# Routing logits transposed, attention logits by two blocks, and a software pipeline written out at both ends

## What is computed

```python
x = x + attention(layernorm(x))
x = x + slots(layernorm(x))
# attention, per batch
q    = tanh(x @ W_charge.T + b);  shell = normalised(x @ W_shell.T + b)
phi  = (powers 0..4 of q, outer product with cos/sin of shell @ omega.T) @ W_combine.T   # 64 features
attn = softmax(causal(phi @ phi.T * decay / temp));  out = attn @ V @ W_out.T
# slots, per batch
h      = gelu(concat(x, slot_mean) @ w1.T + b1)
logits = (h @ w2.T + b2) / (|tau| + 0.1)            # 64 per token
alpha  = softmax over the 8 largest of the 64, 0 elsewhere
S_new  = GRU(alpha.T @ x / sum(alpha), slots);  out = alpha @ (S_new @ wv.T + bv) @ wo.T
```

## Time and profile before

| what | us |
|---|---|
| median of 3 runs (809.03 to 813.24) | 812.28 |
| the profiled execution's own time | 810.81 |
| its span, first to last instruction | 809.0 |
| PE busy | 736.9 (91%) |
| DVE busy | 614.1 (76%) |
| ACT busy | 438.8 (54%) |
| POOL busy | 420.4 (52%) |
| mean granted clock of TensorE | 0.969 of full speed |

### The profile page before, as it was taken

One profiled execution on the slowest core, in us unless ns is written; L12 is line 12 of the kernel. 1 busy time (PEld: TensorE's weight loads), 2 busy tenths in 40 slices (PEclk: granted clock), 3 DMA queues, 4 the chain that ended last, 5 costly groups with the idle time before them and its releaser, 6 DMA issues.

```text
span 809.0 us, 14937 instructions
## 1 busy us (share of the span) xinstructions
PE 736.9 (91%) x4448; PEld 584.9 (72%) x4448; DVE 614.1 (76%) x2069; ACT 438.8 (54%) x870; POOL 420.4 (52%) x681
## 2 busy tenths in 40 slices
PE   4647799999999999999999999999999999989952
PEld 2535576878778787878787787878787877767742
DVE  1653769697888979797979889797979798866642
ACT  0414648383847656473838475664737384727310
POOL 1433465656473837566564738374665557361410
PEclk9978999999999999999999999999999999999976
DMA  8015352535463544546454535445464645262133
GB/s 288 6 34 123 79 131 53 131 91 145 116 144 106 133 140 111 166 105 184 92 144 124 141 113 127 145 112 155 106 182 97 167 108 151 53 156 77 57 104 104
DMA packets 80104, 97.11 MB, mean 120 GB/s; under 512 B 12118, under 2 KB 54680, under 8 KB 80024
## 3 DMA queue, kind: packets, MB, share of 16 engines
q1 hardware_dynamic: 75760, 92.95, 44.6%
q10 hardware_dynamic: 4264, 3.20, 1.3%
HBM read 20.62 MB, written 16.78 MB: 46 GB/s over the span
## 4 chain that ended last, share of the span: by engine, by line
PE 67%; DVE 8%; DMA 5%; POOL 5%; SPq 5%; ACT 5%; issue 4%; ACTq 0%; POOLq 0%; DVEq 0%
PE ps L341 13%; PE ps L262 13%; PE ps L236 12%; PE ps L367 6%; PE ps L408 4%; PE ps L297 3%; PE ps L393 3%; POOL Z L1079 2%; PE ps L314 2%; DMA X<-in_x 2%; SPq L1244 2%; DMA out_x<-X 2%; PE ps L316 2%; PE ps L230 2%; PE ps L379 2%
## 5 line engine op out<-in xcount | busy, mean ns | idle before, releaser
L341 PE MATMUL ps<-VS,ET 128*128 128x257 f32 x640 | 160.3, 389 | 0.0
L341 PEld LDWEIGHTS ps<-VS,ET 128*128 128x128 f32 x640 | 114.3, 191 | 25.5 <-DVE X L803 10.5
L610 ACT ACTIVATE E<-ps,nmax 128x128 f32<-128x128 f32 (+3 forms) x128 | 66.2, 532 | 86.1 <-DVE nmax L791 85.5
L726 DVE TENSOR_TENSOR VS<-ps,biasM 128x354 f32<-128x354 f32 x128 | 67.0, 524 | 42.2 <-PE ps L262 40.2
L1079 POOL TENSOR_TENSOR Z<-Z,QB 128x512 f32<-128x512 f32 x64 | 81.7, 1276 | 32.0 <-ACT Z L591 29.3
L549 ACT ACTIVATE xn<-X,rs 128x256 f32<-128x256 f32 x128 | 66.3, 590 | 40.1 <-POOL rs L1029 39.9
L262 PE MATMUL ps<-W1h,xh 128*128 128x354 f32 x256 | 86.5, 338 | 0.7 <-DVE xl L715 0.7
L262 PE MATMUL ps<-W1h,xl 128*128 128x354 f32 x256 | 83.6, 326 | 0.0
L262 PE MATMUL ps<-W1l,xh 128*128 128x354 f32 x256 | 83.3, 325 | 0.0
L631 ACT ACTIVATE xmT<-ps 128x512 f32<-128x512 f32 x64 | 36.7, 608 | 78.9 <-PE ps L236 78.9
L791 DVE TENSOR_REDUCE nmax<-ps 128x1 f32<-128x128 f32 (+3 forms) x128 | 60.6, 483 | 21.3 <-PE ps L318 21.0
(11 more groups left out here) (176 smaller groups left out, 1873.7 us busy)
## 6 DMA issues: line engine op xcount, KB each, us to landing
X<-in_x SPq DMA_DIRECT2D x32, 512.0 KB, 4.8
xmT<-Z SPq DMA_DIRECT2D x128, 128.0 KB, 2.3
out_x<-X SPq DMA_DIRECT2D x32, 512.0 KB, 3.6
QS<-Z SPq DMA_DIRECT2D x64, 128.0 KB, 2.4
KH<-Z SPq DMA_DIRECT2D x64, 128.0 KB, 2.4
KL<-Z SPq DMA_DIRECT2D x64, 128.0 KB, 2.4
AS<-grz SPq DMA_DIRECT2D x32, 128.0 KB, 2.4
AS<-aTl SPq DMA_DIRECT2D x32, 128.0 KB, 2.4
```

What stands on the lines that cost most here:

```text
L341: ins = e.matmul(p[:, 0:D + 1], ET[:, r % 2, j * 128:j * 128 + 128], VS[:, (2 * k + d) % 4, j, 0:D + 1], start=j == 0, stop=j == i)
L610: e.activation(E[:, r % 3, 0:w], at["lg", r][:, 0:w], ACT.Exp, bias=nmax[:, r % 8:r % 8 + 1]).then_inc(s["E"], 1)
L726: e.tensor_tensor(VS[:, b % 4, t, :], at["vs", b, t][:, 0:FEATS], biasM[:, :], ALU.add).then_inc(s["vs"], 1)
```

## The change

- **Routing.** `route` is one step for a pair: w2 is stationary and the hidden layer moves, two matmuls with 512 columns, one to each half of the partitions. `rt_out` (ACT) adds the bias, `rt_t` (PE) transposes the result with four transposes into a bank of ring T. `top` and `shift` read the logits there; `route_logits` is gone. `shift` of the logits moves from POOL to DVE, and that of the 8 maxima stays on POOL (`shift8`).
- **Attention logits.** `logits(k, n)` makes two blocks: four fp32r matmuls, then two mask matmuls.
- **phi.** The last two matmuls use all 128 rows, with weights `w4` in which one half is zero.
- **Norms.** The DVE's bn_aggr instructions (16 for a pair) go; `ln_scale` and `lm_scale` join the two halves that bn_stats leaves, with four more small POOL instructions in each.
- **Order.** All sequences are new. The loop runs over `range(3, NP - 1)`; what comes before and after it is written out. The first batches' statistics stand ahead of the weight setup on DVE, the first transposes ahead of the bias setup on PE; the loads of the slot layer move from ACT's queue to SP's.
- A few waits and small forms are added or changed.

```diff
-        SETUP, SOFT, CHAIN, SLOTS = 9, 9, 5, 12
+        SETUP, SOFT, CHAIN, SLOTS = 7, 9, 5, 12
...
-                    ins = e.matmul(p[own(d), :], wc[own(d), 2, :], Z[own(d), 4, :], start=False, stop=True)
+                    ins = e.matmul(p[own(d), :], w4[:, d, :], Z[:, 4, :], start=False, stop=True)
...
             def logits(k, n):
+                for r in (8 * k + 2 * n, 8 * k + 2 * n + 1):
+                    at["lg", r], before = L.take(s["E"], r + 1)
+                    if before:
+                        e.wait_ge(*before)
                 if n == 0:
                     e.wait_ge(s["qk"], 192 * (k + 1))
+                for u in (2 * n, 2 * n + 1):
+                    d, i = divmod(u, 4)
+                    rows, wide = slice(i * 128, i * 128 + 128), max(i * 128 + 128, 256)
+                    p = at["lg", 8 * k + u]
+                    for j, keys in enumerate((KH, KL)):
+                        e.matmul(p[:, 0:wide], QS[:, d, rows], keys[:, d, 0:wide], start=j == 0, stop=False,
+                                 skip_group_check=True)
+                for u in (2 * n, 2 * n + 1):
+                    i = u % 4
+                    e.matmul(at["lg", 8 * k + u][:, i * 128:i * 128 + 128], identb[:, :], maskb[:, :], start=False,
+                             stop=True, skip_group_check=True).then_inc(s["lg_mm"], 1)
...
-                for t in range(4):
-                    ins = e.matmul(p[:, t * S:t * S + S], hT[:, d, t * 128:t * 128 + 128], w2[:, :],
-                                   start=True, stop=True, skip_group_check=True)
+                e.wait_ge(s["h"], 2 * k + 2)
+                for d in range(2):
+                    ins = e.matmul(p[own(d), :], w2[:, :], hT[:, d, :], start=True, stop=True)
                 ins.then_inc(s["rt_mm"], 1)
+            def rt_t(k):
+                p, before = T.take(s["dm"], 2 * k + 2)
+                e.wait_ge(s["rtT"], k + 1)
+                transposes(p, [RT[:, t * 128:t * 128 + 128] for t in range(4)]).then_inc(s["rt_t"], 1)
...
+            def rt_out(k):
+                e.wait_ge(s["rt_mm"], k + 1)
+                e.activation(RT, at["rt", k][:, :], ACT.Identity, bias=b2[:, 0:1]).then_inc(s["rtT"], 1)
...
+                e.tensor_tensor(lg[:, d, 0, :, :], logits_of(k, d),
+                                m8[:, d, :, 0:1].broadcast_to([128, 4, S]), ALU.subtract).then_inc(s["dm"], 1)
...
+            for it in range(3, NP - 1):
+                p, n, f, m, g = it + 2, it + 1, it, it - 1, it - 2
+                e_t(f, 5); values(f, 4); xn_t(p, 0, 0); e_t(f, 6); values(f, 5); xn_t(p, 0, 1); phi(n)
+                e_t(f, 7); values(f, 6); values(f, 7); xn_t(p, 1, 0); xn_t(p, 1, 1); out_mm(g, 0, 0)
+                proj(p, 0, 0); out_mm(g, 0, 1); gather(m); proj(p, 0, 1); out_mm(g, 1, 0); proj(p, 0, 2)
+                proj(p, 0, 3); proj(p, 1, 0); proj(p, 1, 1); out_mm(g, 1, 1); proj(p, 1, 2); proj(p, 1, 3)
+                logits(n, 0); gi_t(m); xm_t(f, 0, 0); xm_t(f, 0, 1); gx_rz(m); logits(n, 1); e_t(n, 0)
+                e_t(n, 1); gx_n(m); q_t(p); xm_t(f, 1, 0); xm_t(f, 1, 1); hidden(f, 0); hidden(f, 1)
+                values(n, 0); al_t(m); logits(n, 2); route(f); values(n, 1); z_t(p); e_t(n, 2); slot_v(m)
+                rt_t(f); values(n, 2); e_t(n, 3); e_t(n, 4); logits(n, 3); values(n, 3)
```

More of the change, by code:

```diff
@@ L83 @@
 ln_r ln_b
+rt_t rtT wcast
+ln_d ln_e ln_q lm_d lm_e lm_q
 """.split()
@@ new lines, in _ @@
+            e_t(1, 2); logits(1, 2); values(1, 1); xm_t(0, 1, 0); xn_t(3, 0, 1); e_t(1, 3); xm_t(0, 1, 1)
+            values(1, 2); hidden(0, 0); hidden(0, 1); z_t(2); e_t(1, 4); values(1, 3); logits(1, 3)
+            route(0); proj(3, 0, 0); values(1, 4); rt_t(0); e_t(1, 5); proj(3, 0, 1); e_t(1, 6); phi(2)
+            values(1, 5); proj(3, 0, 2); proj(3, 0, 3); xn_t(3, 1, 0); e_t(1, 7); values(1, 6)
+            xn_t(3, 1, 1); values(1, 7); proj(3, 1, 0); proj(3, 1, 1); proj(3, 1, 2); logits(2, 0)
@@ new lines, in _ @@
+            gather(0); xm_t(1, 0, 0); proj(3, 1, 3); gi_t(0); e_t(2, 0); logits(2, 1); gx_rz(0); q_t(3)
+            values(2, 0); e_t(2, 1); xm_t(1, 0, 1); gx_n(0); e_t(2, 2); logits(2, 2); xm_t(1, 1, 0)
+            xm_t(1, 1, 1); hidden(1, 0); hidden(1, 1); logits(2, 3); al_t(0); route(1); values(2, 1)
+            e_t(2, 3); rt_t(1); values(2, 2); z_t(3); e_t(2, 4); slot_v(0); values(2, 3); xn_t(4, 0, 0)
+            values(2, 4); e_t(2, 5); xn_t(4, 0, 1); xn_t(4, 1, 0); e_t(2, 6); values(2, 5); e_t(2, 7)
@@ new lines, in _ @@
+            phi(3); proj(4, 0, 0); proj(4, 0, 1); values(2, 6); xn_t(4, 1, 1); proj(4, 0, 2); proj(4, 0, 3)
+            out_mm(0, 0, 0); values(2, 7); xm_t(2, 0, 0); out_mm(0, 0, 1); proj(4, 1, 0); proj(4, 1, 1)
+            proj(4, 1, 2); proj(4, 1, 3); logits(3, 0); gather(1); out_mm(0, 1, 0); out_mm(0, 1, 1); q_t(4)
+            xm_t(2, 0, 1); gi_t(1); logits(3, 1); gx_rz(1); e_t(3, 0); xm_t(2, 1, 0); xm_t(2, 1, 1); gx_n(1)
+            hidden(2, 0); hidden(2, 1); values(3, 0); e_t(3, 1); e_t(3, 2); logits(3, 2); al_t(1)
```

497 lines of the change are left out of this document (308 added, 189 removed).

## The result

The changed kernel takes 780.12 us (median of four runs, 776.68 to 782.99), the kernel before 810.65 in the same session (808.04 to 813.24). The ratio is 0.962, with a 95% interval from 0.957 to 0.968: 3.8% faster, and 3 us from the predicted 777. The profiled execution of after took 776.68 us with a span of 774.9, that of before 810.81 with 809.0, so the spans differ by 34.1 us, where the prediction's terms sum to 35. After's profiled execution is the fastest of its four, so what is read from its trace describes a time 3.4 us under the median.

What follows compares the result with a forecast made beforehand. PE work was taken to bound the middle (44.24 us a turn), latencies both ends. Middle -15, start -17 and end -3 bring 810.8 to 775.8; the median stands 1.5 above, so 777 us, range 768 to 786 (chance 0.50).

Steps and rivals of the forecast that it cites:

- The start: Up to the logits of pair 1: earlier statistics and transposes, `proj` woven into idle PE time; -17 us.
- the weaving of `proj(2)`: Between the logits of pairs 0 and 1: `proj(2)` fills idle PE time in pair 0's attention; 6 us.
- Rival D: At the start: latencies of one pair are only moved, -7 in place of -17, 787 us; chance 0.12.
- Rival B: Middle turns lose their short gaps too, 1.7 us each, and the start gives 24: 761 us; chance 0.15.
- Sum: -1.05 us a pair: PE work in a middle turn: fp32r entries -0.63, routing -0.36, phi -0.06, masks and the rest 0.
- the price of 0 for the gaps of the old turn: Middle turns on PE: old gaps against waiting for two ring L banks, 0, between -0.8 and +0.8 a turn.
- the terms of phi and of the routing: PE in a middle turn: phi's last two matmuls -0.06 us, routing from 1.8 to 1.44, -0.36.
- The entries: PE in a middle turn: seven fewer switches into fp32r at 0.09 us each, -0.63.
- The bank wait: `e_t(f, 5)` on PE waits for ring T's bank until DVE's `shift`; 0.8 us of room, priced 0, up to 3.
- Rival C: Middle: DVE reaches `top` late by more than 0.8 us, holding up PE every turn; slower, 829 us; chance 0.06.
- Ring L's two banks: Two-block logits on PE wait for two free banks instead of one; 0, between -0.8 and +0.8 a turn.
- The end: Last pair: `gather` goes ahead of `out_mm` and starts 2.5 us sooner; -3 in all, between -6 and +3.

Runs made afterwards that it cites:

- this mixture: Changed kernel with the routing part and phi's last two matmuls in their old forms, in the new order: 793.7 us, ratio 0.979 to before.
- the dose: Changed kernel with four unused reductions on DVE ahead of `top`, 2.3 us more DVE time a turn: 796.0 us, ratio 0.983 to before.
- the last experiment: Changed kernel with `z_t` ahead of the slot setup's rest and some first- and last-pair moves issued from ACT's queue: 779.1 us, ratio 0.961 to before.

## Why the prediction was right, and where two errors met

**The sum and its parts.** From the start to the logits of pair 1: forecast -17, measured 118.06 to 102.01, -16.1. From there to the logits of pair 15: forecast -15, measured 609.3 to 593.6, -15.7. From there to the end: forecast -3, measured 81.7 to 79.3, -2.4. The single marks at the start were right as well: logits of pair 0 at 67.6 for 69, of pair 1 at 102.0 for 101. Of the first 100 us PE idles for 26.9 (38.4 before), where about 20 were forecast.

**The start** came about by the mechanism given. The experiment with the old order gave 12.6 us at phi of pair 0, some 2 of them by slow first matmuls (forecast about 8 to 10 for the step). The logits of pair 0 come 13.0 us sooner (forecast 11), and from there to the logits of pair 1 only 3.1 us went (37.5 to 34.5), where the weaving of `proj(2)` was given 6. Two errors of 2 and 3 us meet in the -16.1. Rival D is out. Rival B had 24 for the start: the first 85 us still have 27 us idle, and the logits of pair 0 wait 4.4 for the keys.

**The middle was right only in its sum.** The step that failed is "Sum: -1.05 us a pair", and of it above all the price of 0 for the gaps of the old turn; the terms of phi and of the routing were mis-sized. By the mean of the eleven turns a turn lost 1.70 us, of which 1.66 is recorded busy time. Counted from each start to the next, or to the record's own end where that comes first, it splits like this:

| part, us a turn | before | after | change | forecast |
|---|---|---|---|---|
| fp32r work and `hidden` (logits, `out_mm`, `proj`) | 16.96 | 16.22 | -0.74 | -0.63 |
| masks | 0.92 | 0.58 | -0.34 | 0 |
| `route` and `rt_t` | 1.73 | 1.45 | -0.28 | -0.36 |
| phi | 2.87 | 2.73 | -0.14 | -0.06 |
| all other | 21.50 | 21.34 | -0.16 | 0 |

`hidden` is in the first row because a block's first matmul starts inside the record that stands ahead of it. Half of the last row is eight transposes of the normalised input fewer in this stretch. The entries came out nearly as forecast. The masks are the same in number, but two in a turn were followed by a wait. PE in order of time before, twice the same two operations:

```profile
292.55 0.23 PE L318 MATMUL ps<-maskb,identb 128*128 128x128 bf16 x1
292.90 0.30 PE L236 MATMUL ps<-ident,E 128*128 128x128 f32 x1
...
308.20 0.23 PE L318 MATMUL ps<-maskb,identb 128*128 128x128 bf16 x1
308.27 0.28 PE L236 MATMUL ps<-ident,E 128*128 128x128 f32 x1
```

The transpose follows the lone mask after 0.35 in one place and after 0.07 in the other. The difference is a wait that the modelled end of the mask's record covers, so that it counts as busy. With the like one ahead of `q_t` (0.20) that makes 0.42 a turn. In after no mask has one; ahead of `route` the mask pays 0.09 for the narrow form. This is rival B's mechanism (the short gaps that lone blocks left, a turn of 1.7 less), and in the middle rival B was nearer than the forecast. The routing gained 0.28, and less the 0.09 ahead of it 0.19, half of its term: the prediction looked for the price of the narrow form between the two halves of phi (0.06) and not in the operation ahead of them.

Undone in the new order the parts measured, in the commonest turn: route 0.6, phi 0.1, norms 0.7, the place of the masks 0.3. These are not shares of the 1.7. The old loop had bn_aggr on DVE and no wait for it, so the norms' 0.7 is what the new order would lose with it, and half of route's 0.6 is two short waits that only this mixture has.

What hid the error is the other side: the forecast took all fourteen turns as equal. In the three turns from phi of pair 1 to that of pair 4 there is now 4.2 us more idle PE time than before (6.9 in all: keys of the next pair twice, 2.0; the bank of `rt_t`, 1.7; z's transfer, 1.5; low halves on DVE, 1.5), and the stretch is 2.7 us longer. Some 1.6 us of work is in it that was not before: six matmuls of `values` (0.22 each) and three transposes of the probabilities (0.11 each), since less of them now stands ahead of phi of pair 1. Eleven turns of -1.7 and three of +0.9 make the -16 that fourteen of -1.05 were to make. That the sum came out right is luck.

**The bank wait** was there as described, and priced rightly: 0.6 us of room instead of 0.8, the rest of the dose paid in full, and in after it shows once. Rival C needed 3.3 us of lateness; DVE, rid of `bn_aggr`, is in time (busy for 35.7 us a turn, 37.5 before; forecast 35; POOL 27.4 for 25.7, forecast 29.5). With `bn_aggr` back it isn't, but at another place (`aTl`).

**Ring L's two banks**, "price this at 0, between -0.8 and +0.8": in the new order no wait for the pair of banks in the eleven turns, and the old gaps gone, which is inside the bound at its fast side; in the old order 1.6 a turn, outside of it. The bound came from the gaps of the old turn, which say nothing on how long two banks are occupied; that would have had to be read from `expo` and `row_max` against PE's own order.

**The end** gained 2.4 for 3. `gather` came where it was forecast. Behind it the chain is still SP's queue, and the last experiment shows that 3 to 5 us of it can be had.

The single longer turns of the new order are waits for transfers: in after's turn of 44.0 PE waits 0.73 us for alpha's low part and 0.67 for z. Why the transfers are late there, and what the two short waits of the kernel with `route` in its old form are for, stays open.

## What to carry to other kernels

Price an operation change in the order in which it will stand. In this kernel each of three changes that save PE or DVE work made it 2.6 to 9% slower where it was put into the old order; with all of them in the new order it is 4% faster than before, and undoing the parts that were tested there costs 0.1 to 0.7 us a turn. When a step is moved, look on every queue for what it depends on: the transfer behind `z_t` waited for the very work that `z_t` had been moved past. And where a sum comes out right, compare its parts: here fourteen equal turns stood for eleven that gained more and three that lost. An engine that is recorded as busy for 99% can still have short waits: they show when the same two operations stand at different distances.
